# The seventh stage's causal mask and unit matrix in the rounded 32-bit format in place of bf16

## The reference, cut to what matters

```
qp = q @ Wq.T
kv = latent_kv @ Wkv_expand.T
k, v = jnp.split(kv, 2, axis=-1)
...
scores = jnp.einsum('bhqd,bhkd->bhqk', qh, kh) * inv_sqrt_d
causal = jnp.tril(jnp.ones((sq, sk), dtype=bool))
scores = jnp.where(causal, scores, jnp.finfo(scores.dtype).min)
attn = jax.nn.softmax(scores, axis=-1)
out = jnp.einsum('bhqk,bhkd->bhqd', attn, vh)
```

## Time and profile before

| what | value |
|---|---|
| median of 3 runs | 4189.95 us (4176.59 to 4193.37) |
| the profiled execution, its own time | 4168.21 us |
| its span, first to last instruction | 4166.5 us |
| busy: PE, PEld, DVE, ACT, POOL | 68%, 52%, 61%, 40%, 15% |
| mean granted TensorE clock | 0.804 |
| first and last mask matmul start at | 2819.8 and 3381.5 us |

### The profile page before, as it was taken

The page is one execution under the profiler, slowest core; times in us unless marked ns, Lnnn a source line. Parts: engine busy times, 40 slices in busy tenths (PEclk is TensorE's granted clock), DMA queues, the critical chain, the costliest instruction groups (busy, mean ns, idle before and its releaser), DMA issues.

```text
span 4166.5 us, 42971 instructions
## 1 busy us (share of the span) xinstructions
PE 2818.8 (68%) x12708; PEld 2164.6 (52%) x12708; DVE 2546.0 (61%) x4354; ACT 1667.4 (40%) x3214; POOL 619.7 (15%) x2159
## 2 busy tenths in 40 slices
PE   3330705133320667989989899449999965999999
PEld 2220504132220555656656566337787754888887
DVE  5679697887889524655656556554555454444443
ACT  1118182645579012434434344114454422333332
POOL 0006051423336000000000000002222212000000
PEclk7565857566665866999989899557999977999999
DMA  3000000000000043111111111000000004222332
GB/s 137 11 7 0 0 0 0 0 0 0 0 12 0 15 169 150 66 62 39 68 49 61 56 49 43 7 33 3 1 1 1 1 21 150 93 97 94 109 109 74
DMA packets 50122, 186.12 MB, mean 45 GB/s; under 512 B 6428, under 2 KB 7708, under 8 KB 42852
## 3 DMA queue, kind: packets, MB, share of 16 engines
q1 hardware_dynamic: 47460, 176.37, 11.8%
q0 software_dynamic: 2560, 8.42, 0.5%
HBM read 162.72 MB, written 22.05 MB: 44 GB/s over the span
## 4 chain that ended last, share of the span: by engine, by line
PE 37%; issue 28%; DVE 5%; ACT 2%; POOL 1%; DMA 1%; POOLq 0%; SPq 0%; ACTq 0%; DVEq 0%; PEldq 0%
PE ps L87 11%; PE ps L89 10%; PE ps L88 10%; DVE c_junks L1014 2%; PE ps L1760 2%; ACT c_junks L166 1%; PE ps L1749 1%; PE ps L1602 1%; PE ps L1622 1%; PE ps L1549 0%; PE ps L1550 0%; POOL h_sorted L549 0%; DVE h_junk L1320 0%; PE ps L136 0%; PE ps L1804 0%
## 5 line engine op out<-in xcount | busy, mean ns | idle before, releaser
L166 ACT ACTIVATE b_junk_high<-b_z,b_tk 128x2048 bf16<-128x2048 f32 x208 | 414.7, 1994 | 208.3 <-POOLq L172 147.9
L158 DVE TENSOR_SCALAR_CACHE_REDUCE b_junk_low<-b_z,b_tk 128x2048 bf16<-128x2048 f32 x208 | 471.8, 2342 | 1.7 <-POOLq L175 1.7
L1501 PE MATMUL ps<-ident,b_z 128*128 128x128 f32 x256 | 43.6, 343 | 559.9 <-DVEq L921 533.4
L1501 PEld LDWEIGHTS ps<-ident,b_z 128*128 128x128 f32 x256 | 40.4, 183 | 563.8 <-DVEq L921 535.1
L649 ACT ACTIVATE e_p<-ps,e_st 128x512 f32<-128x512 f32 x256 | 175.9, 687 | 253.2 <-DVE e_st L1062 253.2
L1078 DVE TENSOR_TENSOR e_pT_lo<-ps,e_pT_hi 128x512 fp32r<-128x512 f32 x256 | 175.2, 686 | 132.4 <-ACT e_pT_hi L659 132.4
L130 POOL TENSOR_TENSOR ln_rstd<-ln_var,minus_half 128x4 f32<-128x4 f32 x24 | 24.7, 1029 | 1543.5 <-DVE ln_var L115 1520.7
L1062 DVE TENSOR_REDUCE e_st<-ps 128x1 f32<-128x512 f32 x256 | 175.7, 686 | 113.3 <-PE ps L89 106.2
L136 PE MATMUL ps<-ident,xn 128*128 128x128 f32 x320 | 72.7, 420 | 243.6 <-DVE xn L118 243.6
L530 POOL TENSOR_SCALAR g_p<-g_p,g_st 128x128 f32<-128x128 f32 (+3 forms) x256 | 131.3, 532 | 444.7 <-DVE g_st L1249 444.7
L136 PEld LDWEIGHTS ps<-ident,xn 128*128 128x128 f32 x320 | 65.3, 225 | 252.6 <-DVE xn L118 252.6
(11 more groups left out here) (460 smaller groups left out, 8719.5 us busy)
## 6 DMA issues: line engine op xcount, KB each, us to landing
h_w<-in_l_blob SPq DMA_DIRECT2D x80, 512.0 KB, 3.6
e_g<-e_g_kept SPq DMA_DIRECT2D x32, 1024.0 KB, 4.8
e_qkw<-e_qkw_kept SPq DMA_DIRECT2D x32, 640.0 KB, 5.7
h_w<-in_l_blob SPq DMA_DIRECT2D x80, 256.0 KB, 2.6
e_g_kept<-e_g SPq DMA_DIRECT2D x8, 1024.0 KB, 5.9
e_blob<-in_l_heads SPq DMA_DIRECT2D x4, 1728.0 KB, 9.3
e_p<-in_l_heads SPq DMA_DIRECT2D x4, 1728.0 KB, 9.2
e_qkw_kept<-e_qkw SPq DMA_DIRECT2D x8, 640.0 KB, 3.0
```

The costliest lines, as they stand in the source:

```text
L158: dve.tensor_scalar(junk[j], data[:, j, :], cand[:, j:j + 1], 0.0, ALU.is_ge, ALU.add, accum_out=cnt[:, j:j + 1])\
L166: act.activation(junk[j], data[:, j, :], ACT.Sign, bias=cand[:, j:j + 1], accum_out=cnt[:, j:j + 1])\
```

## The change

The two tiles take the format `F32R`, four bytes an element, in place of bf16, two bytes. Everything else is the same text: the two copies that fill them now write 32 bits, and the 256 mask matmuls read both operands in 32 bits. No instruction, wait or transfer is added, taken away or moved.

```
         g_mask = m("g_mask", [P, P])
-        g_mask_b, g_ident_b = m("g_mask_b", [P, P], mybir.dt.bfloat16), m("g_ident_b", [P, P], mybir.dt.bfloat16)
+        g_mask_b, g_ident_b = m("g_mask_b", [P, P], F32R), m("g_ident_b", [P, P], F32R)
         g_st = m("g_st", [P, 3, 12])
```

## The result

The changed kernel takes 4214.13 us (median of 5 runs, 4212.71 to 4228.54). The kernel before, now with 5 runs, has a median of 4176.59 us (4166.76 to 4193.37). The ratio is 1.0089, with a 95% interval of 1.0056 to 1.0121: slower by 0.9%, some 37 us. The two intervals overlap; the change costs some 0.9 to 1.2%.

The account below looks back on a forecast made before the run. TensorE was taken to bound the mask's stage; 30 us of mask loads plus 22 us of clock falls gave 52 us, 4168.2 to 4220 on the profiled execution and 4242 us for the median, range 4208 to 4268.

Parts of the forecast that it names:

- the likeliest case: Seventh stage: the longer mask load is paid and some 8 to 22 more clock falls come, 4224 to 4258 us; chance 0.62.
- the load alone: Mask matmuls: the longer load is paid and the clock stays as granted, 4220 us (4210 to 4225); chance 0.20.
- TensorE bounds the stage, no cover: Stretch 2810 to 3390 us: TensorE busy 574.84 of 580 us, so time added to its queue is added to the kernel.
- The count of waits: Stretch 2810 to 3390 us: TensorE waited for another engine three times, the longest 2.1 us.
- Filling copies and stream at 0: The two copies filling the tiles and streaming the mask's 128 columns in 32 bits were taken to add 0 us.
- Entering the mask, gain 0: Step from last score load to mask load: its stall of some 0.15 us comes from the change of rows and stays.
- rival B: Before the mask: the stall is due to the format and goes, giving back 38 us, about 4182 us; chance 0.05.
- The mask's load, 30 us: The 256 mask weight loads: 216 x 0.103 + 40 x 0.23 = 31 us, taken as 30.
- rival C: Mask weight load: the rounded 32-bit format loads as fast as bf16, nothing changes, 4190 us; chance 0.05.
- The granted clock, 22 us from 15 more falls: Score stretches: longer light time brings 15 more clock falls at 1.5 us each, 22 us.
- The sign that I named: Changed trace of the stage: a mean clock of 0.86 or lower against 0.89 before.
- The base: Whole kernel: the unchanged time of 4190 us to which the forecast 52 us were added, giving 4242.

Follow-up runs that it names:

- experiment 1: Kernel before plus, ahead of each bf16 mask matmul, one matmul with a 32-bit unit matrix and two columns of zeros: 4237.28 us, ratio 1.0148.
- Grouping: Kernel before with the masks of blocks 1 to 3 issued together after block 3's scores: bf16 4111.13 us, ratio 0.9858; 32 bits 4155.05 us, ratio 0.9966.
- the two profiles: The changed kernel profiled in two separate comparisons with the kernel before: ratio 1.0089 in the first, 1.0121 in the second.
- the last comparison: The changed kernel measured again, unaltered, beside the kernel before on the same chip: 4231.85 us, ratio 1.0121.

## Why the prediction was right, and where its terms were off

The range (4208 to 4268) holds the time, and the direction was right. The mechanism of the likeliest case, the load in the open plus more falls of the clock, is what happened. Its number is not: 4214 lies below that case's band (4224 to 4258) and inside that of the load alone (4210 to 4225), and the range holds it because it takes in both. Step by step:

- **TensorE bounds the stage, no cover.** Right: the added time arrived whole, with TensorE busy for 597.6 of 598.2 us. VectorE's later start cost nothing. The count of waits was misread: between 2810 and 3390 us of the kernel before TensorE waits four times, on three kinds of row, 5.1 us in all.
- **Filling copies and stream at 0.** Right: the copy of the unit matrix takes 0.29 us still (here is its row after; ScalarE's timeline), and experiment 1 shows the load alone at full price, with at most 0.03 us left for 128 columns of stream.

```profile
2803.83 0.29 ACT L719 ACTIVATE g_ident_b<-ident 128x128 fp32r<-128x128 f32 x1
```

- **Entering the mask, gain 0.** Right: 0.26 us before and after, and over all masks at the full clock a median of 0.320 and 0.321. Grouping shows that the stall goes with the change of rows, in either format. The prediction's rival B is out.
- **The mask's load, 30 us.** The mechanism is right, the size a little too large. At the full clock the rows of before gave 256 x 0.103 = 26 us; 23.9 and 23.5 were measured in the two profiles, 0.096 us a mask. The 4 us that I added for the half clock took 40 masks there and 0.23 us each. Only 27 of the masks of before and 24 of the changed kernel's start at the half clock, and the step out of the mask shows 0.18 there (0.40 against 0.22), not 0.23: the row that stood for the 32-bit load was not one of this mask's. (In the split above, what a mask loses to the half clock counts with the clock.) The Trainium skill's measured factor of 2 for the fast load (page "TensorE: Matmul & The Clock Gate", section "Weight-path perf modes — Fast Weight Load (FWL) and DoubleRow") would give, as an estimate, 256 x 0.054 = 14 us. The trace shows more: from a bf16 mask's load to a next load on the same rows pass 0.006 us, in 32 bits 0.108. The prediction's rival C, the fast load kept for the rounded format, is out: 186 ns, as every other 32-bit load.
- **The granted clock, 22 us from 15 more falls.** Right in kind, uncertain in size: 15.0 us in the first profile and 32 in the second (70 us more at the half level x 0.46). By all runs of the last comparison it is 56 x 0.46 = 26 us. My 22 lies between, but not by its own working. The record has 25 unbroken spells at the half clock in the stage before, where I had 37, and 34 and 37 after: 9 and 12 more, not 15. A spell lasts 4.7 us on average before (4.4 and 5.1 after), not 3.5, so it costs some 2.2 us, not 1.5 (and the rows that gave 1.5 give 8.3 - 6.7 = 1.6). Too many falls at too low a price came out near the middle, which is luck. The sign that I named, a clock of 0.86 or lower, failed in the first profile (0.87) and held in the second (0.85). The case in which the load alone is paid (A, 4220) would also have fitted the first median of 4214 by its number, but the stage's split rules it out: its half-clock time grew in both profiles.
- **The base.** I put the sum on the median of three, 4189.95; more runs moved the kernel before to 4177, 4174, 4170 and 4183 us in four comparisons. Of the 28 us by which 4242 was too high, 13 are the base's; the difference forecast, 52 us, stands against 37 and 49 measured. On a base of 4177 the same terms give 4229, 15 us too high, and the likeliest case's band would start at 4211 and hold the time.

## What to carry to other kernels

In this kernel nothing hides the weight load of a small matmul that stands between matmuls on other rows of the array, so the format of its stationary operand is paid in full: 0.10 us a matmul, 24 us in all. The same kernel shows the larger lever beside it: issue such matmuls together, so that the rows change less often (59 us gained by moving a few lines). And read a stage's time in two parts, at the full clock and by the clock: with the clock at 0.89, every edit but the doubled bf16 mask moved the stage by 1.2 to 2.4 times its price at the full clock.

## What the runs showed of the hardware that was not expected

Work can be added for nothing: 256 further matmuls of 14 us at the full clock left the kernel at 1.0006 of its time, as the stage spent 79 us at the half clock in place of 118. Removing light work paid more than its price: without the masks 60 us go at the full clock and 107 in all. Why the same bf16 matmul gives time back behind a bf16 mask and not behind a 32-bit one was not settled; that the stretches then are too light either way would fit, but no run here tests it.
